# Output products of the cross attentions from split factors, half of the queries kept in memory, and two edits in the experts

## The reference

```python
q_hk = (hidden_q @ Wq.T).reshape(b, s, H, K)
q_big = einsum('bshk,hkq->bshq', q_hk, w_kc_q)        # rotated in the second layer
kv_r = rope(kv_c)
scores = einsum('bhsr,bhlr->bhsl', q_big @ W_qr, kv_r @ W_kr)
ctx_c = einsum('bhsl,bld->bhsd', softmax(scores), kv_r)
ctx_lat = einsum('bhsd,hkd->bhsk', ctx_c, w_kc_kv)
out = ctx_lat.transpose(0, 2, 1, 3).reshape(b, s, H * K) @ Wo.T
```

## Time and profile before

| | us |
|---|---|
| median of 3 runs | 2145.6 |
| lowest, highest | 2142.59, 2147.81 |
| profiled execution, its own time | 2146.89 |
| its span | 2145.1 |
| mean granted clock of PE in it | 0.981 |

### The profile page before, as it was taken

How to read it: one execution, slowest core, us unless ns; L and a number is a source line. 1 busy time by engine, 2 the same in 40 slices (tenths; PEclk the granted TensorE clock), 3 DMA queues, 4 the chain that set the end, 5 groups by cost and what they waited for, 6 DMA issues and landing times. The chain is left out here.

```text
span 2145.1 us, 27878 instructions
## 1 busy us (share of the span) xinstructions
PE 2035.0 (95%) x8746; PEld 1371.8 (64%) x8746; DVE 1163.7 (54%) x2698; ACT 798.7 (37%) x1986; POOL 955.7 (45%) x929
## 2 busy tenths in 40 slices
PE   7999999998999999999998999999978999999995
PEld 6867676686588744666656676667654555555552
DVE  4258888366561122555547788759863434444442
ACT  2354443143411200333335434335524444445441
POOL 1265573211252100577768656366303444555552
PEclk9999999999999999999999999999987999999998
DMA  5220011300211100111122000110344999888886
GB/s 195 99 80 23 23 28 39 80 2 1 100 58 53 34 1 0 32 50 41 55 88 63 25 21 25 63 67 1 104 150 138 307 301 327 211 215 210 215 208 167
DMA packets 83391, 209.19 MB, mean 98 GB/s; under 512 B 13728, under 2 KB 39840, under 8 KB 74752
## 3 DMA queue, kind: packets, MB, share of 16 engines
q1 hardware_dynamic: 60528, 153.54, 20.8%
q0 software_dynamic: 21280, 51.38, 11.7%
q10 hardware_dynamic: 1440, 2.49, 0.3%
HBM read 257.95 MB, written 34.36 MB: 136 GB/s over the span
## 5 line engine op out<-in xcount | busy, mean ns | idle before, releaser
L98 PE MATMUL banks<-L1f_w,L1f_xT 128*128 x760 | 265.3, 492 | 2.6 <-issue 1.3
L2673 POOL DMA_INDIRECT moe_sums<-L1f_y,L1f_row x95 | 150.6, 1585 | 221.6 <-DVE L1f_is_who L2542 150.6
L159 POOL TENSOR_TENSOR rstd<-rstd,power 128x1 f32<-128x1 f32 x48 | 28.6, 596 | 399.3 <-DVE rstd L153 399.3
L98 PEld LDWEIGHTS banks<-L1f_w,L1f_xT 128*128 128x128 f32 x760 | 138.0, 192 | 83.1 <-issue 7.8
L2681 POOL DMA_INDIRECT L1f_xg<-moe_rows,L1f_row x95 | 94.2, 991 | 64.8 <-DVE L1f_row L2537 37.7
L2509 DVE SCALAR_TENSOR_TENSOR L1f_z<-banks,L1f_share,L1f_sg 128x192 f32<-128x192 f32 x95 | 39.7, 418 | 148.5 <-ACT L1f_sg L2444 148.4
L461 PE MATMUL banks<-L0x_wn,L0x_qT 128*128 128x512 f32 x256 | 115.1, 593 | 0.8 <-DVE x L531 0.8
L461 PE MATMUL banks<-L1x_wn,L1x_qT 128*128 128x512 f32 x256 | 115.1, 593 | 0.8 <-DVE x L531 0.8
L98 PE MATMUL banks<-L0f_down,L0f_z 128*128 128x512 f32 x256 | 111.1, 592 | 1.5 <-DVE L0f_z L2000 1.5
L2444 ACT ACTIVATE L1f_sg<-banks 128x192 f32<-128x192 f32 x95 | 31.4, 330 | 206.9 <-PE banks L98 206.9
L98 PE MATMUL banks<-L0f_hT_hi,L0f_ug_hi 128*128 128x512 f32 x256 | 100.0, 391 | 0.0
(11 more groups left out here) (402 smaller groups left out, 5258.5 us busy)
## 6 DMA issues: line engine op xcount, KB each, us to landing
L1f_w<-in_experts SPq DMA_DIRECT2D x95, 1280.0 KB
L1f_laid<-moe_counts SPq DMA_DIRECT2D x59, 512.0 KB, 5.4
w<-in_L1x_heads SPq DMA_DIRECT2D x16, 704.0 KB, 4.0
w<-in_L0x_heads SPq DMA_DIRECT2D x8, 1216.0 KB, 5.2
w<-in_wug SPq DMA_DIRECT2D x8, 1024.0 KB, 4.8
L0x_craw<-in_ctx SPq DMA_DIRECT2D x96, 64.0 KB, 2.1
L1x_craw<-in_ctx SPq DMA_DIRECT2D x96, 64.0 KB, 2.0
w<-in_L0x_out SPq DMA_DIRECT2D x4, 1280.0 KB, 5.6
```

Of the source, the lines that this page charges most:

```text
L98: ins = pe.e.matmul(out, w, m, start=first and n == 0, stop=last and n == len(pairs) - 1)
L159: pool.e.tensor_tensor(self.rstd[:, i:i + 1], self.rstd[:, i:i + 1], self.power[:, 0:1], ALU.pow).then_inc(self.rstd_set.sem, 1)
L2673: pool.e.indirect_dma_start(self.sums[j % 2][:, :], bass.IndirectOffsetOnAxis(ap=self.row[:, j:j + 1], axis=0), self.y[j % self.NY][:], No ...
```

## The change

In both cross attentions:

- `wn` is kept as two halves (ACT the high one, DVE the low one, `folded_lo`), and the folds ahead of the loop go round four banks instead of two.
- Each part of the output product takes its context in two halves. ACT makes the high one (`split_hi`, one turn ahead), DVE the low one (`split_lo`, in the turn of the product, behind `find_peak` and `weigh`), and PE does three one-pass matmuls for each of the four heads. PE waits for both halves of part b-7 in turn b.
- The context of b-3 is written by ACT (`keep_context`) instead of DVE.
- `qT` holds four tiles. The queries of the other four go through two small buffers to memory, a DMA for each pair of heads (L0x) or head (L1x), and come back tile by tile from turn 12 on, when the tile whose place they take has had its product. The exponentials of batch 1 wait for all sends, since they overwrite the buffers; a score waits for its tile's return.
- The split of the next stage's weights is spread over the last turns on ACT and DVE. In the second self attention POOL clears one tile ahead and four within its own first turn; in the first, as before.
- SP waits for the end of the cross attention behind the self attention's loads.

In the experts: the first five steps of the limits alternate between two pairs of banks; and the last block isn't added in memory, but spread by matmuls with a matrix that has a one where a token's row is, from the two halves of its output, and added by DVE, while the tensors of the earlier blocks are read, the even one first.

The core of the diff, in the order LatentAttention, the two query stages, SelfAttention, Experts:

```diff
-        self.qT = self.sb("qT", [P, NT, XH, P])
+        with ExitStack() as part:
+            self.qT = self.sb("qT", [P, self.HALF, XH, P], F32, part)
+        self.ctx_lo = self.sb("ctx_lo", [P, self.HALF, XH, P], F32R)
...
+    def fold_bank_of(self, h):
+        return self.sh.psum((3, 6, 4, 5)[h % 4])
+    def folds_kept(self, eng, n):
+        eng.wait_ge(self.wn_hi, n)
+        eng.wait_ge(self.wn_lo, n)
...
+            if b >= 12 and b % BPT == 0 and b // BPT - 3 < self.HALF:
+                self.take_back(sp, b // BPT - 3)
...
+    def take_back(self, sp, i):
+        self.sent_all(sp)
+        sp.wait_ge(self.projected, BPT * (i + 1))
+        sp.wait_ge(self.q_back, 16 * i)
+        sp.e.dma_start(self.qT[:, i, :, :], self.far[:, :, i * P:(i + 1) * P]).then_inc(self.q_back.sem, 16)
...
+            self.folds_kept(pe, h - 3)
+            self.fold_out(pe, h, self.fold_bank_of(h))
...
+        pe.wait_ge(self.q_back, 16 * (b // BPT - self.HALF + 1))
...
     def project_out(self, pe, i, part):
+        o = BPT * i + part
         if part == 0:
             pe.wait_ge(self.x_set, i)
-        pe.wait_ge(self.wn_set, XH)
-        pe.wait_ge(self.ctx_set, (i + 1) * BPT)
-        for h in range(4 * part, 4 * part + 4):
-            ins = pe.e.matmul(self.o_bank, self.qT[:, i, h, :], self.wn[:, h, :], start=h == 0, stop=h == XH - 1)
-        if part == BPT - 1:
-            ins.then_inc(self.projected.sem, 1)
+        self.folds_kept(pe, XH)
+        pe.wait_ge(self.part_hi_set, o + 1)
+        pe.wait_ge(self.part_lo_set, o + 1)
+        both = (self.part_hi[o % 2][:], self.part_of(self.ctx_lo, o))
+        accumulate(pe, self.o_bank, [p for n in range(4) for p in parts(
+            cut(both, slice(None), slice(n * P, (n + 1) * P)), cut(self.wn, slice(None), 4 * part + n))],
+            first=part == 0, last=part == BPT - 1).then_inc(self.projected.sem, 1)
...
+            if 0 <= b - self.LAG_VALUES < B:
+                self.keep_context(act, b - self.LAG_VALUES)
             if b < B:
...
+            o = b - self.LAG_VALUES - BPT + 1
+            if 0 <= o < BPT * NT:
+                self.split_hi(act, o)
+            if o > self.LAST and o < self.LAST + BPT:
+                self.after.halves_hi(act, o - self.LAST - 1)
+    def split_hi(self, act, o):
+        act.wait_ge(self.ctx_set, BPT * (o // BPT + 1))
+        act.wait_ge(self.projected, o - 1)
+        act.e.copy(self.part_hi[o % 2][:], self.part_of(self.qT, o)).then_inc(self.part_hi_set.sem, 1)
+    def keep_context(self, act, b):
+        act.wait_ge(self.mixed, b + 1)
+        act.e.activation(self.of_batch(b), self.c_bank, ACT.Identity,
+                         bias=self.kvT[b % self.NKT][:, LC * P:LC * P + 1]).then_inc(self.ctx_set.sem, 1)
...
+        if b == 1:
+            self.sent_all(act)
...
+        for h in range(self.FIRST):
+            self.folded_lo(dve, h, self.fold_bank_of(h))
         for b in range(B + self.LAG_VALUES + BPT):
             if b < B:
                 self.find_peak(dve, b)
             if 0 <= b - 1 < B:
                 self.weigh(dve, b - 1)
-            v, t = b - self.LAG_VALUES, b - self.LAG_TURN
-            if 0 <= v < B:
-                dve.wait_ge(self.mixed, v + 1)
-                dve.e.tensor_scalar(self.of_batch(v), self.c_bank, self.kvT[v % self.NKT][:, LC * P:LC * P + 1], None,
-                                    ALU.add).then_inc(self.ctx_set.sem, 1)
+            o, t = b - self.LAG_VALUES - BPT, b - self.LAG_TURN
+            if o >= 0:
+                self.split_lo(dve, o)
...
             if 0 <= t < B:
                 for c in range(LC):
                     hi, lo = cut(self.pT[t % 2], slice(None), c)
                     dve.wait_ge(self.pT_hi, 2 * t + c + 1)
                     dve.e.tensor_tensor(lo, self.t_bank[:, c * BANK:(c + 1) * BANK], hi, ALU.subtract).then_inc(self.pT_lo.sem, 1)
-            o = b - self.LAG_VALUES - BPT
-            if o == self.LAST:
-                self.after.halves_lo(dve)
...
+            if self.FIRST + b < XH:
+                self.folded_lo(dve, self.FIRST + b, self.o_bank)
+            if self.LAST <= o < self.LAST + BPT - 1:
+                self.after.halves_lo(dve, o - self.LAST)
             if o >= 0 and o % BPT == BPT - 1:
                 i = o // BPT
-                dve.wait_ge(self.projected, i + 1)
+                dve.wait_ge(self.projected, BPT * (i + 1))
                 dve.e.tensor_tensor(self.sh.x[:, i, :], self.sh.x[:, i, :], self.o_bank, ALU.add).then_inc(self.x_set.sem, 1)
                 dve.wait_ge(self.x_set, i + 1)
                 self.next_statistics(dve, i)
+        self.after.halves_lo(dve, BPT - 1)
...
+    def folded_lo(self, dve, h, bank):
+        hi, lo = cut(self.wn, slice(None), h)
+        dve.wait_ge(self.wn_hi, h + 1)
+        dve.e.tensor_tensor(lo, bank, hi, ALU.subtract).then_inc(self.wn_lo.sem, 1)
+    def split_lo(self, dve, o):
+        dve.wait_ge(self.part_hi_set, o + 1)
+        dve.e.tensor_tensor(self.part_of(self.ctx_lo, o), self.part_of(self.qT, o), self.part_hi[o % 2][:],
+                            ALU.subtract).then_inc(self.part_lo_set.sem, 1)
...
+    def send(self, sp, g):
+        sp.wait_ge(self.q0_set, 2 * g + 2)
+        sp.wait_ge(self.q1_set, 2 * g + 2)
+        sp.e.dma_start(self.far[:, 2 * g:2 * g + 2, :], self.away[g % 2][:]).then_inc(self.sent[g % 2].sem, 16)
...
+    def q_cols(self, eng, g, t, e):
+        if t:
+            eng.wait_ge(self.sent[g % 2], 16 * (g // 2))
+            return self.away[g % 2][:, e, :].rearrange("p (i n) -> p i n", n=P)
+        return self.qT[:, :, 2 * g + e, :]
...
+                self.send(sp, h - 3)
+        self.sync_attention(sp, XH - 3)
...
+    def send(self, sp, h):
+        sp.wait_ge(self.q_set, 2 * h + 2)
+        sp.e.dma_start(self.far[:, h, :], self.away[h % 2][:]).then_inc(self.sent[h % 2].sem, 16)
...
-    def halves_hi(self, act):
+    def halves_hi(self, act, n):
+        w, dst, width = self.w[n], (self.w_q, self.w_k, self.w_v)[n], (D, self.kw, self.vw)[n]
...
-                self.input_hi(act, n)
-    def halves_lo(self, dve):
-        self.normalise(dve, 0)
...
+    def halves_lo(self, dve, step):
+        if step == 0:
+            self.normalise(dve, 0)
+            self.normalise(dve, 1)
+        elif step == 1:
+            self.begin_early(dve)
+            self.input_lo(dve, 0)
+        elif step == 2:
+            self.weights_lo(dve, 0, self.w_q, D)
+        else:
+            self.input_lo(dve, 1)
+            self.weights_lo(dve, 2, self.w_v, self.vw)
+    def weights_lo(self, dve, n, dst, width):
...
         self.begin_early(pool)
-        for tile in (*self.kbd, *self.vbd[0:2]):
+        for tile in self.clear_early:
             pool.e.memset(tile[:], 0.0).then_inc(self.cleared.sem, 1)
...
+        self.begin(sp)
...
     def gpsimd(self, pool):
         self.begin(pool)
-        pool.e.memset(self.vbd[2][:], 0.0).then_inc(self.cleared.sem, 1)
         for i in range(NT + 5):
             if i < NT and self.normed:
...
                 pool.e.tensor_tensor(self.tiny[:, i, 2:4, :], self.tiny[:, i, 0:2, :], half, ALU.pow).then_inc(self.norm_root.sem, 1)
+            if i == 0:
+                for tile in self.clear_late:
+                    pool.e.memset(tile[:], 0.0).then_inc(self.cleared.sem, 1)
...
+    def limit_banks(self, j):
+        return self.sh.psum(6 if j < self.AHEAD and j % 2 else 0, 2)
...
+        sp.wait_ge(self.counts_kept, 16)
+        sp.e.dma_start(self.tri[:], d["numbers"]).then_inc(self.numbered.sem, 16)
+        sp.wait_ge(self.added[0], 16 * self.adds(0))
         for i in range(NT):
             sp.e.dma_start(self.sh.x[:, i, :], self.sums[0][i * P:(i + 1) * P, :]).then_inc(self.even_back[i].sem, 16)
+        sp.wait_ge(self.added[1], 16 * self.adds(1))
+        for n, signal in enumerate(self.odd_back):
+            sp.e.dma_start(self.h[:, 2 * n:2 * n + 2, :], self.sums[1][2 * n * P:(2 * n + 2) * P, :].rearrange(
+                "(i p) n -> p i n", p=P)).then_inc(signal.sem, 16)
...
+    def spread_last(self, pe):
+        pe.wait_ge(self.goes_to, 1)
+        pe.wait_ge(self.last_hi, 1)
+        pe.wait_ge(self.last_lo, 1)
+        pe.wait_ge(self.y_set, self.LAST)
+        for i in range(NT):
+            places = self.upto[:, i * P:(i + 1) * P]
+            accumulate(pe, self.sh.psum(i), [(places, part) for part in self.last_parts()]).then_inc(self.by_row.sem, 1)
...
-        pe.wait_ge(self.seen, j)
+        if j == 1:
+            pe.wait_ge(self.planned, 3)
+        pe.wait_ge(self.seen, j - 1 if j < self.AHEAD else j)
...
+        act.wait_ge(self.y_made, self.BLOCKS)
+        act.e.copy(self.last_parts()[0], self.y_bank(self.LAST)).then_inc(self.last_hi.sem, 1)
...
-        dve.wait_ge(self.odd_back, 16)
+            if j == self.LAST - 2:
+                self.find_goal(dve)
+        hi, lo = self.last_parts()
+        dve.wait_ge(self.last_hi, 1)
```

(56 more changed lines are left out.)

122 lines of the change are left out of this document (61 added, 61 removed).

## The result

The changed kernel takes 2255.5 us (median of 4 runs, 2250.96 to 2256.55), the kernel before 2146.65 us (4 runs): a ratio of 1.0507, interval 1.0486 to 1.0528. That is 109 us more. The profiled execution has a span of 2254.1 us.

The account below looks back on a forecast made before the run. PE was taken to bound the kernel, DVE next. Ring +85, clock +35, attention ends 0, clears +3, experts' head -3 and tail -6 sum to +114 us on the median of 2145.6: 2260 us, range 2200 to 2305.

Parts of the forecast that it names:

- Part 1, the product: Output product in the cross attentions: 12 matmuls 0.23 us apart take 2.76 us instead of 3.43, 0.67 us less each.
- Part 2, the wait: Cross attention turns b = 7 to 31: PE waits 2.37 us for DVE's low half, net 1.70 x 50 = +85 us.
- the row: Profile row of L2051, two SBUF inputs, 675/685/1781 ns: its median, taken against POOL contention, gave a split of 0.85 us.
- Part 3, the clock: PE's gaps in the cross attentions lower the clock in half of 50 turns at 1.4 us: +35 us, ends 0 and +68.
- the upper end: Highest clock cost in the cross attention turns: 40 dips x 1.7 us = +68 us.
- Part 4, the ends: Fills, last tiles, query transfers of the attentions: 0, ends -5 and +5 each; second self attention's clears +3 us.
- the fill: Turns before b = 7, without a product: DVE loses L518 in four, gains seven folded_lo; 0 (-2 to +3).
- Queries' sends and reloads: Queries of four tiles go to memory and back in the cross attentions, reloads asked about 50 us ahead: 0.
- Part 5, the experts: Experts: -3 us at the head from alternating banks, -6 (-3 to -7) at the tail from spreading the last block.
- the held clock: Rival for the cross attentions: same waits, no clock dips, 2145.6 + 85 - 6 = 2225 us; chance 0.25.
- the right ring: Cross attention turns: PE waits for DVE's low half, behind maxima needing PE's score; next score queues behind that wait; +85 us.
- The hidden wait: Rival: DVE reaches the split before PE turned its weights, 64 products save 0.67 us each, 2097 us; chance 0.08.

Follow-up runs that it names:

- the kernel with the later root: Changed kernel with DVE making the low half one turn ahead, plus POOL taking the root for a tile's statistics one turn later: 2118.2 us, ratio 0.9869.
- the one with two-input scalings: Changed kernel with DVE scaling the probabilities by two multiplications of two SBUF inputs instead of four scalings with one: 2256.1 us, ratio 1.0518.
- the other waits mended: Low half one turn ahead, POOL's root later, ACT's fill context and last high half reordered, POOL's clears spread, on the changed kernel: 2106.3 us, ratio 0.9823.

## Why the prediction was right, point by point

Forecast 2260, measured 2255.5 us, with the mechanism that was named, and its signs are there: 54 waits of 109.7 us in sum (110 to 120 forecast, for some 50), PE at 31 to 33 of 40 us (30), scores 10.3 us apart on the mean (near 10). The terms, though, were off in both directions, and that the sum came within 5 us is in part luck: the two loops with their clock cost 97 us for a forecast of 120, and the fills, the last tiles and the clears 18 more than forecast. (The range's lower end takes 18 us off for the ends; the lowest values given with the last tiles and the experts alone add up to 22.5.)

**Part 1, the product.** 0.67 us less for each was exact: where nothing is waited for, a turn lasts 7.60 us against 8.27, in 21 turns in a row of the kernel with the later root.

**Part 2, the wait.** Forecast 2.37 us a turn. With nothing in the way the product starts 4.26 us after the score, in the changed kernel 7.29, 7.07, 6.07 and 5.37 us after it: 3.03, 2.81, 1.81 and 1.11 late, mean 2.19. The waits of the table are 0.2 to 0.3 shorter, because a record's modelled end reaches into the wait. The forecast gave 0.18 us a turn too much. In batches 16 to 19 DVE comes to the low half 6.25, 5.24, 4.55 and 6.27 us after the score, mean 5.58 for the 5.77 taken from the kernel before: the larger of the two misses. The split takes 0.73 us on the mean of these four (0.68 three times, 0.88 once), for 0.85; the signal takes 0.15 for 0.10, and PE is ready at 4.26 instead of 4.35. In sum (2.19 - 0.67) x 48 = 73 us for the 48 turns of the table, where the forecast gives 82. By the rule cited there (the Trainium skill, GPSIMD Engine Reference, Key points) a split beside POOL's work is held up. The traces agree with it, against what I made of the row: in the changed kernel 15 of 15 low halves that start while a POOL instruction runs take 0.88 to 1.48 us, in the one with two-input scalings the median is 1.07 in the first attention and 1.21 in the second. Of L2051 in the kernel before, too, the long ones (1.1 to 1.8 us) are those that start while POOL runs L2051 or L2072, and beside nearly all of the short ones POOL had nothing running. So the median of that row is that of a DVE left alone and said nothing against the rule. The number came out near since in two turns of four POOL isn't working at that place, in a third it usually comes just behind, and in the fourth only 0.2 us of its instruction are left.

**Part 3, the clock.** Forecast a fall in half the turns at 1.4 us, 35 us. There were 14 in the 48 turns, 9 of them in the turn after the short one and 2 in the first turn with a product, of 1.4 to 1.6 us each, 22 in sum; 73 + 22 = 95 of the 97 us measured. The size of one was right, the count too high. Gaps of 0.9 and 1.6 us never did it, one of 2.85 did not, one of 2.68 did, and of ten gaps of 2.8 us (2.77 to 2.79) one did not, so the last gap alone doesn't decide. The Trainium skill (TensorE: Matmul & The Clock Gate, "A second HAM failure mode: psum-queue depth-cycling") tells of a clock that swings through short idles; the trace agrees that it does here, at three turns in ten, far from the upper end.

**Part 4, the ends.** The forecast of 0 for the fill was wrong: +4.6 and +2.8. Two steps failed. One is the sentence that the exponentials, 1.3 us later, are needed only in the next turn. On ACT the high halves of the turned probabilities stand behind them, and PE waited 1.26 us in each of turns 4 to 7 of the first attention and 5 to 7 of the second (before, 0.86 in some of them). The other is that DVE's work in the fill is about even. Its amount may be, but a fold of the loop goes into the bank of the one before, and now waits until DVE has made the low half of that one, behind the scalings of the turn, where it had waited for ACT's copy alone: PE waited 0.9 and 1.0 us for it in turns 1 and 2 of both attentions, where before it waited 0.17 in one of them.

```profile
134.83 1.10 PE L449 MATMUL banks<-w 128*128 128x512 f32 x2 [0.94 <-DVE L0x_wn_lo L603]
...
139.63 1.10 PE L449 MATMUL banks<-w 128*128 128x512 f32 x2 [1.00 <-DVE L0x_wn_lo L603]
...
152.59 0.47 PE L98 MATMUL banks<-L0x_pT_hi,L0x_kvs_hi 128*128 128x512 f32 x1 [1.26 <-DVE L0x_pT_lo L587]
```

With the context behind the exponentials the wait of turns 5 to 7 fell to 0.4. The second fill is then as long as before the change (42.5 for 42.6 us), the first, at 42.0, still 4.2 longer than the 37.8 before it: the waits for the folds stayed in both (1.0, and 1.9 or 1.6 us), no run takes them away, and what they cost is open. In the last tile both waits that were named came, 2.61 us for the low half of part 28 in both attentions, 2.01 and 3.43 for that of part 31, and in both a stretch at the lower clock at each, which was not in the sum: +3.4 and +4.5 instead of 0. (These two rows of the table also hold the wait of turn 31, 2.2 us, which the forecast has among its 50.) Queries' sends and reloads cost +0.6 and nothing. L1a got 6.1 us longer instead of 3, and 4 of them went with the clears apart: POOL was not late, it held up DVE.

**Part 5, the experts.** -9.4 for -9, but not from the same places. Head (from L1a's last sum to the first turned rows): 34.1 to 30.5 us, -3.6 for -3. The blocks -1.9, not forecast. The tail, from the last block's output to the end, -4.0 for -6:

```profile
2233.88 0.59 ACT L2620 CAST L1f_member<-banks 128x512 fp32r<-128x512 f32 x1 [2.15 <-PE banks L2587]
...
2240.10 3.96 DVE L2693 TENSOR_TENSOR x<-x,banks 128x512 f32<-128x512 f32 x6 [2.64 <-DMA x<-moe_sums]
2244.65 5.31 DVE L2697 TENSOR_TENSOR x<-x,L1f_h 128x512 f32<-128x512 f32 x8 [0.59 <-DMA L1f_h<-moe_sums]
```

From the last block's output to the last add 16.1 us, before 19.4, forecast 13: the condition "if the reads of the sums are there" didn't hold, DVE waits 2.64 and 0.59 us for them.

Of the rivals, the held clock at 2225 us named the right ring and missed the 22 us of the clock. The hidden wait gave 2097 us, by running the low half ahead of the maxima; with DVE in that order the kernel is at 2135.6 us, and with the other waits mended at 2106.

## What to carry to other kernels

A shorter instruction on the bounding engine is worth nothing if its new operand is made behind work that waits for that engine's own step in the same turn: list what stands ahead of the operand on its engine, and make it earlier (here 120 us for moving one instruction within its turn, 125 for making it one turn ahead). When the ring is gone, look for the next wait at once; here each of the next ones, a root on POOL and a copy on ACT, was again one of order, and worth 4 to 12 us. A gap on PE costs its clock as well, but part of that is only a later wait that comes sooner.

## What the runs showed of the hardware

POOL and DVE hold each other up inside instructions, and it is the one that is running when the other comes that goes first. DVE's scaling of 128x256, with one SBUF input, takes 0.34 us at least and 1.16 at most; its normalisation of 128x512 took 5.32 us beside three clears of POOL, which only write, while a multiplication with two inputs beside such a clear kept its 0.69; the low half, with two inputs, took 0.67 to 1.48 in the first attention, and 2.11 once in the second, behind a POOL instruction of 5.63. POOL's side stretches too: L413, 0.60 us, lasted 1.04 beside the two-input scalings, and L395, 0.73, 1.05. The Trainium skill (SBUF — State Buffer, "Who interferes with whom") says of DVE instructions in a mode that uses two ports, which a `tensor_scalar` can enter, that whoever issues first has the port pair shared with GpSimd for the whole instruction and the other is blocked. The row of 5.32 us agrees, and more sharply than I had used it: DVE did not get its turn between three clears in a row. The clock fell behind 14 of 48 waits of one kernel whose turns mostly repeat to 0.1 us, and behind none between scores 7 and 31 once PE was fed matmuls whose output nobody reads; what decides between two gaps of 2.8 us stays open.
